# Masking the diagonal blocks of a narrow causal attention's first scores: by products on TensorE, or by VectorE while it takes the maxima

## What is computed

```
B, T, D = (2, 512, 512)
H, G = (32, 8)
HD = D // H
...
q = _apply_rope(q)
k = _apply_rope(k)
k = jnp.repeat(k, GROUP, axis=1)
v = jnp.repeat(v, GROUP, axis=1)
scores = jnp.einsum('bhqd,bhkd->bhqk', q, k)
causal = jnp.triu(jnp.ones((t, t), dtype=bool), k=1)
scores = jnp.where(causal, -jnp.inf, scores)
attn = jax.nn.softmax(scores / jnp.sqrt(jnp.float32(HD)), axis=-1)
ctx = jnp.einsum('bhqk,bhkd->bhqd', attn, v)
```

## Time and profile before

| | |
|---|---|
| median of three runs | 3607.86 us (3605.19 to 3608.97) |
| the profiled execution | 3604.55 us, its span 3602.9 us |
| self attention of the second layer in it | from 1950 us to 2410 us, 8 items, some 58 us each |
| PE busy over the span | 91% |
| DVE busy over the span | 54% |
| granted TensorE clock, mean over the span | 0.947 of 2.4 GHz |

### The profile page before, as it was taken

One profiled execution on the slowest core, in us unless ns is written; L12 is line 12 of the kernel. 1 busy time (PEld: TensorE's weight loads), 2 busy tenths in 40 slices (PEclk: granted clock), 3 DMA queues, 4 the chain that ended last, 5 costly groups with the idle time before them and its releaser, 6 DMA issues. The chain is left out here.

```text
span 3602.9 us, 54390 instructions
## 1 busy us (share of the span) xinstructions
PE 3284.9 (91%) x19769; PEld 2511.9 (70%) x19770; DVE 1942.1 (54%) x4740; ACT 1329.2 (37%) x2944; POOL 770.7 (21%) x845
## 2 busy tenths in 40 slices
PE   6999999999999999986985999999999856999998
PEld 6888988887888888863443556555555435777776
DVE  3555665567666666652134455455656545343446
ACT  0444434443444444432112434344555543112121
POOL 1333322222222112214132333342222100000000
PEclk7999999999999999998996999999999978999999
DMA  5221211111111001014441000000000011000001
GB/s 194 54 54 54 54 53 30 36 36 30 30 36 33 21 18 30 24 76 158 136 136 55 3 2 2 8 26 17 8 5 5 2 48 24 24 12 12 12 23 47
DMA packets 110616, 146.80 MB, mean 41 GB/s; under 512 B 23712, under 2 KB 72864, under 8 KB 109288
## 3 DMA queue, kind: packets, MB, share of 16 engines
q1 hardware_dynamic: 95904, 110.80, 9.6%
q0 software_dynamic: 14480, 32.91, 3.0%
HBM read 100.55 MB, written 42.08 MB: 40 GB/s over the span
## 5 line engine op out<-in xcount | busy, mean ns | idle before, releaser
L554 ACT ACTIVATE probs_w<-probs_w,low_w 128x256 f32<-128x256 f32 (+1 forms) x512 | 242.9, 475 | 591.6 <-DVE low_w L599 591.6
L1896 DVE TENSOR_REDUCE mx_n<-bank 128x6 f32<-128x768 f32 (+1 forms) x256 | 279.6, 1092 | 175.6 <-PE bank L1692 111.1
L1823 ACT ACTIVATE probsT_n<-bank 128x768 f32<-128x768 f32 (+1 forms) x256 | 235.6, 920 | 287.0 <-PE bank L1704 287.0
L572 DVE TENSOR_TENSOR probsT_lo_w<-bank,probsT_hi_w 128x384 fp32r<-128x384 f32 (+1 forms) x256 | 159.7, 624 | 124.5 <-ACT probsT_hi_w L537 123.4
L518 PE MATMUL bank<-wo_hi_w,oT_hi_w 128*128 128x512 f32 x512 | 211.8, 414 | 2.1 <-issue 2.1
L518 PE MATMUL bank<-wo_hi_w,oT_lo_w 128*128 128x512 f32 x512 | 204.9, 400 | 0.0
L518 PE MATMUL bank<-wo_lo_w,oT_hi_w 128*128 128x512 f32 x512 | 204.6, 400 | 0.0
L582 DVE TENSOR_SCALAR probs_w<-probs_w,inv_w 128x256 f32<-128x256 f32 (+1 forms) x512 | 188.3, 410 | 20.8 <-issue 0.9
L225 POOL CAST wo_hi_w<-staging_w 128x512 fp32r<-128x512 f32 x64 | 40.0, 624 | 640.6 <-PE bank L518 640.6
L1704 PEld LDWEIGHTS bank<-qT_n,kT_n 50*128 50x128 f32 x1024 | 80.7, 194 | 118.8 <-issue 79.9
L450 PE MATMUL bank<-xT_lo_w,wq_hi_w 128*128 128x512 f32 x512 | 161.8, 397 | 0.0
(11 more groups left out here) (362 smaller groups left out, 8183.2 us busy)
## 6 DMA issues: line engine op xcount, KB each, us to landing
expert_rows<-ctxT_hi_w SPq DMA_DIRECT2D x20, 512.0 KB, 4.8
work_m<-expert_rows SPq DMA_DIRECT2D x40, 256.0 KB, 2.6
expert_products<-work_m POOLq DMA_DIRECT2D x40, 256.0 KB, 2.6
staging_w<-in_L_attn_Wq SPq DMA_DIRECT2D x32, 256.0 KB, 2.9
expert_table<-ctxT_hi_w SPq DMA_DIRECT2D x16, 512.0 KB, 5.7
staging_w<-in_L_attn_Wo SPq DMA_DIRECT2D x32, 256.0 KB, 2.6
staging_w<-in_L_xattn_Wq SPq DMA_DIRECT2D x32, 256.0 KB, 2.6
staging_w<-in_L_xattn_Wo SPq DMA_DIRECT2D x32, 256.0 KB, 2.6
```

The source lines that it names most:

```text
L554: last = act.activation(pr, pr, ACT.Exp, bias=low[:, n % ROUNDS_OF_PROBS, tile:tile + 1], scale=-1.0, accum_out=den[:, n % ROUNDS_OF_PROBS ...
L572: return dve.tensor_tensor(dst, src, hi.bitcast(FP32), ALU.subtract)
L1823: act.activation(probsT[:, turn_ % SLOT_PAIRS, :, 0:cols], scoreT[:, :, 0:cols], ACT.Exp, scale=SCALE)\
L1896: dve.tensor_reduce(to.rearrange("p t h -> p h t"), seen, AX.X, ALU.max).then_inc(s["scores_read"], 1)
```

## The change

DVE masks the diagonal blocks while it takes their maxima, and PE no longer does. For each pair of a self attention item:

- The two mask matmuls go, with `ident16` and `own16` and the two DVE copies that filled them. `scores_ready` is incremented by the last score matmul of each head.
- The one reduction over six blocks (3 for each of 2 heads, 768 elements) becomes a reduction over the two full blocks (256 elements) and four `tensor_tensor_reduce`, one for each diagonal block. Each adds `chip.const[:, C_OWN:...]` (0 or -1e30, in SBUF) to the block, multiplies by -1, writes the 128 results back over the block in PSUM, and takes their minimum into `mx`. Each of them is two instructions, the operation and a read of the accumulator.
- `mx` holds negative maxima for the diagonal blocks. `negate` joins the third with them in one `scalar_tensor_tensor` in place of a `tensor_tensor`, and its sign is turned. It is as many instructions as before.

The cross attention items keep their one reduction.

```diff
                         last = pe.matmul(out, q, kT[half(h, ROWS), n % 2, key_block(n, h), 0:keys],
-                                         start=(t == 0), stop=cross(n), skip_group_check=True)
-                        if cross(n) and t == TILES - 1:
+                                         start=(t == 0), stop=True, skip_group_check=True)
+                        if t == TILES - 1:
                             last.then_inc(s["scores_ready"], 1)
-                if not cross(n):
-                    for h in range(2):
-                        pe.matmul(masked(score[:, h, :]), ident16[:, :], own16[:, :].unsqueeze(1).to_broadcast([P, 2, P]),
-                                  start=False, stop=True, skip_group_check=True).then_inc(s["scores_ready"], 1)
...
                 if cross(n):
                     seen, to = score[:, :, :].rearrange("p h (t k) -> p h t k", t=TILES), mx[:, 0:TILES, at:at + other + 1:other]
+                    dve.tensor_reduce(to.rearrange("p t h -> p h t"), seen, AX.X, ALU.max).then_inc(s["scores_read"], 1)
                 else:
-                    seen, to = score[:, :, 0:3 * P].rearrange("p h (t k) -> p h t k", t=3), mx[:, :, at:at + other + 1:other]
-                dve.tensor_reduce(to.rearrange("p t h -> p h t"), seen, AX.X, ALU.max).then_inc(s["scores_read"], 1)
+
+                    dve.tensor_reduce(mx[:, 2, at:at + other + 1:other], score[:, :, P:2 * P], AX.X, ALU.max)
+                    for h in range(2):
+                        for t in range(TILES):
+                            own = score[:, h, 2 * t * P:(2 * t + 1) * P]
+                            last = dve.tensor_tensor_reduce(
+                                out=own, in0=own, in1=chip.const[:, C_OWN:C_OWN + P],
+                                scale=-1.0, scalar=TOP, op0=ALU.add, op1=ALU.min,
+                                accum_out=mx[:, t, at + other * h:at + other * h + 1])
+                    last.then_inc(s["scores_read"], 1)
...
                 if not cross(n):
-                    dve.tensor_tensor(mx[:, 1, mine_], mx[:, 1, mine_], mx[:, 2, mine_], ALU.max)
+                    dve.scalar_tensor_tensor(mx[:, 1, mine_], mx[:, 2, mine_], -1.0, mx[:, 1, mine_], ALU.mult, ALU.min)
                     dve.drain()
+                sign = -1.0 if cross(n) else 1.0
...
-            dve.tensor_copy(ident16[:, :], chip.ident)
-            dve.tensor_copy(own16[:, :], chip.const[:, C_OWN:C_OWN + P])
```

More of the change, by code:

```diff
@@ L1506, in by_head @@
         return a[:, rotation(name, n) % 2, 0:heads_ * HW].rearrange("p (h w) -> p h w", w=HW)
-    masked = lambda bank: bank.rearrange("p (a b) -> p a b", b=SEQ)[:, :, 0:P]
     with c:
@@ L1903, in negate @@
                 if not cross(n):
[L1904 removed]
+                    dve.scalar_tensor_tensor(mx[:, 1, mine_], mx[:, 2, mine_], -1.0, mx[:, 1, mine_], ALU.mult, ALU.min)
                     dve.drain()
+                sign = -1.0 if cross(n) else 1.0
                 top = mx[:, 0:TILES, mine_]
                 hi, lo = neg_hl[:, i, :, 0:heads_], neg_hl[:, i, :, 16:16 + heads_]
[L1908 removed]
+                dve.tensor_scalar(hi.bitcast(FP32R), top, sign, None, ALU.mult)
                 dve.drain()
[L1910 removed]
+                dve.scalar_tensor_tensor(lo, top, sign, hi, ALU.mult, ALU.subtract)
                 dve.drain().then_inc(s["neg_ready"], 1)
```

3 lines of the change are left out of this document (removed).

## The result

The changed kernel takes 3625.41 us (median of 7 runs, 3615.48 to 3631.59), beside it the kernel before 3607.86 (7 runs, 3600.46 to 3610.18): ratio 1.0050, interval 1.0034 to 1.0066. It is 17.5 us slower, and 27 us above the forecast. The loss is in the self attention of the second layer, which takes 488.6 us in the profiled execution against 460.7; the cross attention behind it takes 468.6 against 466.3, the rest is 3 us shorter. (The profiled execution is the longest of the seven, 3631.6 us, 24 us above the median before. So its rows show more of the loss, and of its time at half clock, than the median has.)

A forecast was written before the change was run, and what follows sets the result against it. PE was taken as the bound only in stretches it works without pause. 1.54 us for each of 8 items gave 12.3 us, less 2.4 for pair 9: 3607.86 - 9.9 = 3598 us, with 8 in 10 for 3585 to 3618.

The forecast's parts named there:

- the six gaining pairs: Pairs 4, 8, 11, 12, 14 and 15, where PE works without pause: together 1.54 us gained per item.
- What PE saves: Dropping the two mask matmuls frees PE 0.22 us per pair, 28 us at most if every pair gained it.
- What DVE pays: Maxima per pair take 1.30 us against 0.96, 0.34 more, at 0.22 per masked block and 0.08 for the last read.
- the mild form of rival 1: Slower PSUM writes, 0.25 us per masked block: 6.7 us cost, 3605 us, no difference; chance 0.20 shared with another rival.
- The loop: PE and DVE alternate in pair 13: DVE's longer maxima use up the earlier start, so the pair stays at 1.87 us.
- Pairs 2, 3 and 9 at zero: No gain or loss: layer norm makes DVE late in 2 and 3 (at worst 0.3 us), POOL sets 9.
- The race in pair 9: DVE's negation may start behind POOL's cast and be held, PE some 0.6 us late; half charged, 0.3 x 8 = 2.4 us.
- The clock: PE's half-clock stretches shift with item length; bad form 14 us slower than forecast, 3612, chance 0.08; helping, 0.12.
- Rival 3: Half-clock stretches after PE's pauses in pairs 9 and 10 change: 3592 to 3576 us (0.12), or 3612 us (0.08).

The follow-up runs named there:

- e10: Changed kernel with the negation for pairs 9 to 11 moved behind pair 10's maxima, in self items only: 3608.6 us, ratio 1.0000 to 1.0019.
- e15: Changed kernel with the masked scores of pair 9 alone written to SBUF, order untouched: 3608.3 us, ratio 1.0002 to 1.0020.
- e1: Changed kernel with all masked scores written to SBUF instead of back into PSUM: 3605.4 us, ratio 0.9987 to 1.0012.
- e5: Changed kernel with the negation for pairs 9 to 11 behind pair 10's maxima, in self and cross items: 3591.7 us, ratio 0.9954 to 0.9977.
- e11: Kernel before with the negation for pairs 9 to 11 behind pair 10's maxima, in self and cross items: 3589.8 us, ratio 0.9946 to 0.9974.
- e3: Changed kernel with PE's two mask matmuls kept, so both engines mask: 3630.8 us, ratio 1.0051 to 1.0091.
- e4: Changed kernel with the transposes of xT1 issued three times in self items, 8 more matmuls: 3617.5 us, ratio 1.0027 to 1.0047.
- e12: Changed kernel, masked scores to SBUF, later negation for pairs 9 to 11, self items' layer norm parts behind the next item's pairs 11 and 12: 3633.1 us.

## Why the prediction was wrong

Two steps failed. The longer maxima were put at nothing in pairs 2, 3 and 9; there item 3 is 1.3 us longer, nearly all that the six gaining pairs bring (1.47). And the second hold in pair 9 was charged 2.4 us in all, without the clock, where removing it gives 14 to 17 (e10, e15).

- **What PE saves** held as a sum: the six pairs that were to gain 1.54 us gain 1.47 from item 3 before to item 3 after, though pairs 12 and 14 gain 0.33 and 0.29 and pairs 4, 8 and 15 only 0.13 to 0.19.
- **What DVE pays** was mis-sized. The step took 0.22 us for each block and 0.08 for the read, from an operation that writes to SBUF, "because the row is the same operation with the same inputs". With PSUM as the target it is 0.25 and 0.14: 1.43 us, not 1.30, 0.47 more than before and not 0.34. That is the mild form of rival 1, priced at "no difference": by itself this term takes 8 x 7 x 0.13 = 7 us. The table in "VectorE: DVE Perf Modes", section on the TRN2 errata, of the Trainium skill had led to an estimate of 1.42 us. Its agreement is luck: its 120 cycles are for a source in PSUM and a target in SBUF, which is e1's case, and e1 took 1.26. (No run writes to another PSUM bank, so whether the write to PSUM as such costs this or the write into the bank that is read stays open.)
- **The loop** of pair 13 was right as a mechanism, and its error is that of the term: 2.01 for 1.87 us.
- **Pairs 2, 3 and 9 at zero** was the costliest step in the plain sum. For pairs 2 and 3 the zero rested on maxima that start earlier by what PE gives, which holds only where they wait for the masks; here they wait for the layer norm, and the pairs are 0.30 and 0.56 us longer. For pair 9 it rested on POOL setting the stretch. But POOL's chain and the maxima both wait for the rotation of `q0`, the maxima start 1.31 us after the first scores before and after, and PE's next first scores wait for their end, so the 0.47 counts in full. Pairs 0, 5, 6 and 13 add 0.63. In e5 against e11, without the double hold, 1.96 us of losses in the item stand against 1.86 of gains (1.54 were forecast): "no change".
- **The race in pair 9** was seen and mispriced. "A difference of 10 ns decides, so I charge half of it" was worked out with maxima of 1.30 us; with 1.43 line 1907 comes 0.13 us behind the cast, in every item. The 0.6 us by which the maxima would be late was near the 0.48 that PE waits, 4 us in all; what failed is that nothing was added for the clock. The rule cited from the Trainium skill ("SBUF — State Buffer", section "Who interferes with whom") fits the holds of lines 1907 and 1914, and the new operations were not held, as it says. Line 1912 (0.86 us in e15) has one SBUF input and was held as well; the same section says so of `tensor_scalar` in its two-port modes, an exception that the prediction left out. No run shows in which mode line 1912 ran.
- **The clock** was a rival with 8% and a price of 14 us in its bad form. In the profiled execution the stage is 27.9 us longer. Eight items at item 3's 0.58 us are 4.6 of it; the rest, 23 us, goes with 73 us more at 1.2 GHz (for the median's 17.5 us the rest would be 13). This part of the loss the sum left out. Rival 3 looked for it in pairs 9 and 10, and e15 shows that this is where it can be removed. But a wait of PE is not always paid in clock: e3 has the longer waits and 61 us at half clock.
- Unsettled: why 0.48 us of wait in pair 10 makes the falls of items 1, 4 and 5 last 10.2 us, and why in items 2 and 6 a stretch of 20.5 us starts behind pair 3. e4 removes the long stretch by filling that pause, e10 and e15 remove it with the pause in place, by their edit in pair 9. So neither pause is its cause alone, and the runs don't say what joins them, nor why e3's longer waits bring a longer fall in one item only.

## What to carry to other kernels

Before work is moved to an engine "with room", list for each of its turns what it waits for: only where it waits for the work that is taken away does its earlier start pay for the longer operation. Where DVE and POOL share a stretch, write down by how many tenths of a us each small DVE operation misses the start of POOL's, since a change of 0.17 us can turn one hold into two. And count the cover that is left: two delays that are free one by one need not be free together, and TensorE may pay for the wait a second time in its clock, as here, or not, as in e3.

## What the runs showed of the hardware

- The same masking operation with its accumulator costs 0.25 us from start to start and 0.14 for the last read when it writes to PSUM, 0.21 and 0.08 when it writes to SBUF (means 320 and 285 ns, 141 and 83 ns); its PSUM source is the same (changed kernel and e1).
- A DVE operation on 2 to 16 numbers takes 0.16 to 0.18 us where it isn't held, and 0.83 to 1.29 us where it started just behind a POOL operation: it then ended with that one (e12, changed kernel). One that starts 0.04 us ahead of POOL's isn't held (e15). In a row of them every second or third is held, as POOL's next operation starts ahead of it (lines 1907 and 1914; lines 130, 135 and 139 in e12).
- TensorE stayed at 1.2 GHz for 20.48 us in which it was busy for 20.47 (changed kernel, item 6).
